# First gather of an expert stage: index from three groups, rows scaled by GpSimd and stored in halves, one score matrix from rounded products

## The reference

```
h = layernorm(x) * (1 + ca) + sa
x = x + ga * attention(h)      # softmax inside segments of 128 rows, plus a global part over segment heads
h = layernorm(x) * (1 + cb) + sb
score = softmax(h @ Wg + bg); expert = argmax; gate = max      # 16 experts, 512 slots each
y = relu(h[slot] @ W1[e] + b1[e]) @ W2[e] + b2[e]
x = x + gb * where(kept, y * gate, 0)      # a token past its expert's 512 slots gives 0
```

## Time and profile before

| what | value |
|---|---|
| three runs | 1816.24 us median, 1816.03 to 1816.32 |
| profiled execution, on the device | 1814.79 us |
| its span, first to last instruction | 1813.2 us |
| mean granted clock of PE | 0.995 of full |
| PE busy | 1779.8 us (98%) |
| PE weight loads busy | 1489.6 us (82%) |
| DVE busy | 1112.3 us (61%) |
| ACT busy | 893.4 us (49%) |
| POOL busy | 610.1 us (34%) |

### The profile page before, as it was taken

How to read it: one execution, slowest core, us unless ns; L and a number is a source line. 1 busy time by engine, 2 the same in 40 slices (tenths; PEclk the granted TensorE clock), 3 DMA queues, 4 the chain that set the end, 5 groups by cost and what they waited for, 6 DMA issues and landing times.

```text
span 1813.2 us, 27903 instructions
## 1 busy us (share of the span) xinstructions
PE 1779.8 (98%) x9135; PEld 1489.6 (82%) x9136; DVE 1112.3 (61%) x1964; ACT 893.4 (49%) x1317; POOL 610.1 (34%) x565
## 2 busy tenths in 40 slices
PE   9999999999999799999999999998998999999998
PEld 5788888888888488898888888888888888888886
DVE  6577887887887644445445444457558675444753
ACT  4446546546546344354444444347467664434741
POOL 1145555555554511123030303043225431304303
PEclk9999999999999899999999999999999999999999
DMA  7586767777777454344453524265446553426522
GB/s 278 183 228 186 197 157 204 180 173 200 188 193 221 95 174 160 112 168 167 144 169 107 174 98 162 98 207 197 158 141 225 197 212 129 155 98 211 201 80 79
DMA packets 148429, 304.09 MB, mean 168 GB/s; under 512 B 18097, under 2 KB 18493, under 8 KB 146326
## 3 DMA queue, kind: packets, MB, share of 16 engines
q1 hardware_dynamic: 115098, 221.01, 35.0%
q0 software_dynamic: 33280, 82.42, 18.8%
HBM read 254.29 MB, written 67.43 MB: 177 GB/s over the span
## 4 chain that ended last, share of the span: by engine, by line
PE 89%; DVE 1%; ACT 1%; issue 1%; DMA 1%; POOL 0%; POOLq 0%; ACTq 0%; DVEq 0%
PE bank L344 27%; PE bank L346 27%; PE bank L345 27%; PE bank L778 3%; PE bank L962 1%; PE bank L875 1%; PE bank L649 1%; PE bank L770 1%; DMA h_rows<-xr 1%; ACT h_f L1304 0%; PE bank L753 0%; ACT h_hi L1303 0%; PE bank L748 0%; DVE w_lo L1746 0%; PE bank L785 0%
## 5 line engine op out<-in xcount | busy, mean ns | idle before, releaser
L1303 ACT ACTIVATE h_hi<-bank,b_col 128x512 fp32r<-128x512 f32 x256 | 176.8, 691 | 526.1 <-PE bank L346 474.9
L1773 DVE TENSOR_TENSOR h_lo<-h_f,h_hi 128x512 fp32r<-128x512 f32 x256 | 174.0, 691 | 349.9 <-ACT h_f L1304 270.7
L344 PE MATMUL bank<-bt_hi,w_hi 128*128 128x512 f32 (+4 forms) x1024 | 359.1, 351 | 3.9 <-DVE w_lo L1746 3.5
L345 PE MATMUL bank<-bt_lo,w_hi 128*128 128x512 f32 (+4 forms) x1024 | 358.0, 350 | 0.0
L346 PE MATMUL bank<-bt_hi,w_lo 128*128 128x512 f32 (+4 forms) x1024 | 358.0, 350 | 0.0
L344 PE MATMUL bank<-w_hi,h_hi 128*128 128x512 f32 x832 | 325.8, 392 | 1.0 <-issue 1.0
L345 PE MATMUL bank<-w_lo,h_hi 128*128 128x512 f32 x832 | 324.2, 390 | 0.0
L346 PE MATMUL bank<-w_hi,h_lo 128*128 128x512 f32 x832 | 323.9, 389 | 0.0
L2069 POOL DMA_INDIRECT out_dram<-yo,tok_x x64 | 75.4, 1178 | 671.7 <-DVE yo L1808 636.4
L344 PEld LDWEIGHTS bank<-bt_hi,w_hi 128*128 128x128 f32 x1024 | 193.2, 189 | 28.8 <-issue 5.6
L345 PEld LDWEIGHTS bank<-bt_lo,w_hi 128*128 128x128 f32 x1024 | 193.3, 189 | 21.2 <-issue 0.2
(11 more groups left out here) (312 smaller groups left out, 2938.0 us busy)
## 6 DMA issues: line engine op xcount, KB each, us to landing
raw<-in_L_ffn_W_dram SPq DMA_DIRECT2D x128, 1024.0 KB
xa<-in_L_attn_x_dram SPq DMA_DIRECT2D x16, 1024.0 KB, 8.5
xr<-in_L_attn_x_dram SPq DMA_DIRECT2D x16, 1024.0 KB, 6.8
xr<-global_rows POOLq DMA_DIRECT2D x16, 1024.0 KB, 8.6
h_rows<-sb_tab SPq DMA_DIRECT2D x16, 1024.0 KB
out_dram<-xr SPq DMA_DIRECT2D x16, 1024.0 KB, 10.7
h_rows<-h POOLq DMA_DIRECT2D x15, 1024.0 KB
b_bc<-in_L_ffn_b_dram SPq DMA_DIRECT2D x16, 256.0 KB, 6.3
```

The lines of the kernel that those rows point to most:

```text
L344: pe.matmul(o, a_hi, b_hi, start=start, stop=False)
L345: pe.matmul(o, a_hi, b_lo, start=False, stop=False)
L1303: act.activation(h1_hi[b % 2][:, j, :], h_bank[j][:, :], ACT.Relu, bias=bias)
L1773: dve.tensor_tensor(h1_lo[b % 2][:, j, :], h1_f[:, j, :], h1_hi[b % 2][:, j, :].bitcast(F32), ALU.subtract) \
```

## The change

Four parts. The score matrix is made from rounded products: ACT rounds each slice of Wk and Wq as it lands, DVE subtracts, PE makes 48 rounded matmuls instead of 16 plain ones, with eight warm-up matmuls instead of six; DVE's splits of M wait for all four copies, since M's parts lie where the rounded Wq lay. The lookup on chip covers Z2, Z1 and Z, so the table's part for expert 0 is loaded before Z2 is scattered, and ahead of SP's last output store; empty entries hold T (8192), and the constants are chosen so that the index is one addition. POOL scales the last group's rows and stores them in two halves, and all scatters of Z2, Z1 and Z follow the first gather. PE makes the ranks of Z1 between two pairs of router quarters.

```diff
     KEY_STEP = 1 << 14
-    FIRST_TAB = 11
-    SPLIT_WV, SPLIT_M, SPLIT_WO, SPLIT_V = 0, KC, 2 * KC, 3 * KC
+    FIRST_TAB = 16
+    NO_TOKEN = T
+    SPLIT_WV, SPLIT_M, SPLIT_WO, SPLIT_V = 2 * KC, 3 * KC, 4 * KC, 5 * KC
...
         load_w2((0, 1), 1)
-        iteration(Group(NG // 2, 0), False, True, False)
-        for par in range(2):
-            sp.wait_ge(scattered[par], 16 * GS * (NG // 2 - 1))
+        sp.wait_ge(scattered[Z3.par], 16 * GS * (Z3.half + 1))
+        sp.wait_ge(scattered[Z2.par], 16 * GS * Z2.half)
...
         sp.dma_start(first_tab[:], slots[:, 0, :, :]).then_inc(first_in, 16)
+        iteration(Group(NG // 2, 0), False, True, False)
...
         pe.wait_ge(ident_made, 2)
-        for _ in range(6):
+        for _ in range(8):
...
         for k in range(KC):
-            pe.wait_ge(wqk_in[k], 32)
+            pe.wait_ge(pro_hi_done, 2 * k + 2)
             for c in range(KC):
-                last = pe.matmul(pro_bank(MCH + c)[:, :], wq_s[:, k, chunk(c)], wk_s[:, k, :],
-                                 start=(k == 0), stop=(k == KC - 1))
+                pe.matmul(pro_bank(MCH + c)[:, :], wq_hi[:, k, chunk(c)], wk_hi[:, k, :], start=(k == 0), stop=False)
+            pe.wait_ge(split_made, 2 * k + 2)
+            for c in range(KC):
+                pe.matmul(pro_bank(MCH + c)[:, :], wq_hi[:, k, chunk(c)], wk_lo[:, k, :], start=False, stop=False)
+                last = pe.matmul(pro_bank(MCH + c)[:, :], wq_lo[:, k, chunk(c)], wk_hi[:, k, :], start=False,
+                                 stop=(k == KC - 1))
...
                 pe.matmul(bank[:, :], ident[:], ga_tab[:, 0, :], start=True, stop=True)
-        def quarters(g):
+        def quarters(g, between=lambda: None):
             for k in range(KC):
+                if k == KC // 2:
+                    between()
...
                 for s in range(GS):
-                    last = pe.matmul(t1_last[:, 0:2 * GS], first_sel[:, which, s, :],
-                                     first_pick[:, which, s, :, :].rearrange("p a j -> p (a j)"), start=(which == 0 and s == 0),
-                                     stop=(which == 1 and s == GS - 1))
-                if which == 1:
+                    for part in range(2):
+                        last = pe.matmul(t1_last[:, 0:GS], first_sel[:, which, s, :], first_pick[:, which, s, part, :],
+                                         start=(which == 0 and s == 0 and part == 0),
+                                         stop=(which == 2 and s == GS - 1 and part == 1))
+                if which == 2:
...
                         last.then_inc(h2t_full, 1)
-            ranks(Z1)
-            quarters(Z)
+            quarters(Z, lambda: ranks(Z1))
...
             first_slots(0)
+            first_slots(1)
             ranks(Z)
-            first_slots(1)
+            first_slots(2)
...
             act.activation(dst, src, ACT.Copy, scale=scale).then_inc(pro_evac, 1)
+        for k in range(KC):
+            act.wait_ge(wqk_in[k], 32)
+            act.activation(wk_hi[:, k, :], wk_s[:, k, :], ACT.Copy).then_inc(pro_hi_done, 1)
+            act.activation(wq_hi[:, k, :], wq_s[:, k, :], ACT.Copy).then_inc(pro_hi_done, 1)
...
         for k in range(KC):
-            act.activation(wv_hi[:, k, :], wv_s[:, k, :], ACT.Copy).then_inc(wv_hi_done, 1)
+            act.activation(wv_hi[:, k, :], wv_s[:, k, :], ACT.Copy).then_inc(pro_hi_done, 1)
...
             dve.memset(quad_sum[k * QUAD:k * QUAD + 1, :], 1.0).then_inc(init_made, 1)
+        for k in range(KC):
+            dve.wait_ge(pro_hi_done, 2 * k + 1)
+            dve.tensor_tensor(wk_lo[:, k, :], wk_s[:, k, :], wk_hi[:, k, :].bitcast(F32), ALU.subtract) \
+                .then_inc(split_made, 1)
+            dve.wait_ge(pro_hi_done, 2 * k + 2)
+            dve.tensor_tensor(wq_lo[:, k, :], wq_s[:, k, :], wq_hi[:, k, :].bitcast(F32), ALU.subtract) \
+                .then_inc(split_made, 1)
...
         for k in range(KC):
-            dve.wait_ge(wv_hi_done, k + 1)
+            dve.wait_ge(pro_hi_done, 2 * KC + k + 1)
...
                 .then_inc(split_made, 1)
+        dve.wait_ge(pro_evac, MCH + KC)
...
             dve.wait_ge(first_step, f + 2)
-            dve.tensor_scalar(first_pick[:, which, :, 0, :], first_tile[:], place[:, 2 * GS:2 * GS + 1], None, ALU.mult) \
+            dve.tensor_scalar(first_pick[:, which, :, 0, :], first_tile[:], place[:, 3 * GS:3 * GS + 1], None, ALU.mult) \
...
         def first_index():
-            dve.wait_ge(first_in, 16)
-            dve.tensor_copy(first_f[:, 0, :], first_tab[:, :, 0]).then_inc(first_step, 1)
-            row, segment = t1_last[:, 0:GS], t1_last[:, GS:2 * GS]
-            shift, whole, total = first_f[:, 1, :], first_f[:, 2, :], first_f[:, 3, :]
             dve.wait_ge(first_full, 1)
-            dve.tensor_scalar(shift, row, 0.0, float(Z1.n * ROWS - 1 - NO_TOKEN), ALU.is_gt, ALU.mult) \
-                .then_inc(first_step, 1)
             dve.wait_ge(first_step, FIRST_TAB)
-            dve.scalar_tensor_tensor(out=whole, in0=segment, scalar=float(P), in1=first_f[:, 0, :], op0=ALU.mult,
-                                     op1=ALU.add).then_inc(first_step, 1)
-            dve.wait_ge(first_step, FIRST_TAB + 2)
-            dve.tensor_tensor(total, row, whole, ALU.add).then_inc(first_step, 1)
-            dve.wait_ge(first_step, FIRST_TAB + 3)
-            dve.tensor_tensor(tok_h[:], shift, total, ALU.add).then_inc(tok_h_ready, 1)
+            dve.tensor_tensor(tok_h[:], t1_last[:, 0:GS], first_f[:, 0, :], ALU.add).then_inc(tok_h_ready, 1)
...
                 first_rows(g, which)
+            if which == 2:
+                dve.wait_ge(first_in, 16)
+                dve.tensor_copy(first_f[:, 0, :], first_tab[:, :, 0]).then_inc(first_step, 1)
...
                 .then_inc(route, 1)
+            if which == 2:
+                first_index()
...
             dve.tensor_tensor(count[:], count[:], osum[:], ALU.add).then_inc(route, 1)
-            if which == 1:
-                first_index()
...
             dve.tensor_tensor(xr[Z.par][:, s, :], xr[Z.par][:, s, :], big[s][:, :], ALU.add).then_inc(x2_ready, 1)
-        def scale_rows(s):
-            dve.wait_ge(xn2_done, 4 * Z.n + s + 1)
-            dve.tensor_tensor(xr[Z1.par][:, s, :], h2[Z.par][:, s, :], cb_tab[:, batch_of(Z), :], ALU.mult) \
-                .then_inc(h2_ready, 1)
...
             half_stats(Z, 2)
-            route_slots(Z2)
-            dve.wait_ge(x2_stored[Z1.par], 16 * (Z1.half + 1))
+            route_slots(Z2, 0)
             route_logits(Z1)
-            for s in range(GS):
-                scale_rows(s)
-            route_slots(Z1, 0)
+            route_slots(Z1, 1)
             route_logits(Z)
-            route_slots(Z, 1)
+            route_slots(Z, 2)
...
             gather(xh, h2_dram, tok_h, xh_in)
-        def store_h2(g, rows=None):
+        def store_h2(g):
...
             stand_alone(pool, pool_passed)
-            rows = h2[g.par] if rows is None else rows
-            pool.dma_start(group_rows(h2_dram, g), rows[:], accum_op=ALU.add).then_inc(h2_stored[g.par], 16)
+            pool.dma_start(group_rows(h2_dram, g), h2[g.par][:], accum_op=ALU.add).then_inc(h2_stored[g.par], 16)
...
                       allow_small_or_imprecise_dtypes=True).then_inc(made, 1)
-            pool.iota(place[:, 0:2 * GS], pattern=[[1, 2 * GS]], base=0, channel_multiplier=0,
+            pool.iota(place[:, 0:3 * GS], pattern=[[P, 3 * GS]], base=Z2.n * ROWS - NO_TOKEN, channel_multiplier=0,
                       allow_small_or_imprecise_dtypes=True).then_inc(made, 1)
-            pool.iota(place[:, 2 * GS:2 * GS + 1], pattern=[[0, 1]], base=1, channel_multiplier=1,
+            pool.iota(place[:, 3 * GS:3 * GS + 1], pattern=[[0, 1]], base=0, channel_multiplier=1,
...
                 pool.tensor_tensor(NR2[:, both], MN2[:, both], RS2[:, both], ALU.mult).then_inc(ln2_rstd, 1)
-            scatter(Z2)
-            store_h2(Z, xr[Z1.par])
-            for par in range(2):
-                pool.wait_ge(h2_stored[par], 16 * (NG // 2))
+            scaled = xr[Z1.par]
+            pool.wait_ge(x2_stored[Z1.par], 16 * (Z1.half + 1))
+            pool.wait_ge(shift_stored[Z.par], 16 * (Z.half + 1))
+            for lo in (0, 2):
+                for s in (lo, lo + 1):
+                    pool.wait_ge(xn2_done, 4 * Z.n + s + 1)
+                    pool.tensor_tensor(scaled[:, s, :], h2[Z.par][:, s, :], cb_tab[:, batch_of(Z), :], ALU.mult) \
+                        .then_inc(h2_ready, 1)
+                pool.wait_ge(h2_ready, 4 * Z.n + lo + 2)
+                pool.dma_start(group_rows(h2_dram, Z)[:, lo:lo + 2, :], scaled[:, lo:lo + 2, :], accum_op=ALU.add) \
+                    .then_inc(h2_stored[Z.par], 16)
+            pool.wait_ge(h2_stored[Z1.par], 16 * (Z1.half + 1))
+            pool.wait_ge(h2_stored[Z.par], 16 * (Z.half + 2))
...
             gather_h(0)
+            pool.wait_ge(first_in, 16)
+            scatter(Z2)
```

14 lines of the change are left out of this document (8 added, 6 removed).

## The result

The changed kernel takes 1833.14 us (median of 5 runs, 1832.17 to 1833.77) against 1816.32 (5 runs, 1816.03 to 1817.07): a ratio of 1.0092, 95% interval 1.0078 to 1.0106. The prediction was 1814.8, with a range up to 1817.2, and gave 5% to "slower". The profiled execution has a span of 1831.6 us and a device time of 1833.14, with PE's mean granted clock at 0.989 of full (0.995 before). The profiled execution of before took 1814.79 us, less than any of its timed runs (1816.03 to 1817.07).

What follows compares the result with a forecast made beforehand. TensorE, busy for 98% of the span, was taken as the bound. Prologue 0 plus tail 1.4 us took the span from 1813.2 to 1811.8 and the median from 1816.24 to 1814.8 us, range 1812.3 to 1817.2.

Steps and rivals of the forecast that it cites:

- Prologue, 0: Rounded score matrix: PE done 2.4 us earlier, all lost waiting for the second modulation matrix; gain 0.
- (b): Prologue rival: the second modulation matrix lands with PE, or earliness pays otherwise; 2.4 + 1.4 us, 1812.4; 6%.
- (d): Prologue loses: DVE late costs up to 1 us, or clock drop costs 2 to 3.4; 1815.3 to 1818.2; 9%.
- What PE gets of it: Before expert 0's transposes: keep-busy starts at 612.6, not 613.31, gather hidden; gain 1.4 us, bounds 0.67 and 2.1.
- Tail, on DVE, and store and gather: Tail: 2.49 us of scaling leaves DVE for POOL, index ready at 611.2, gather at 612.1 instead of 615.65.
- The stores: Tail: second half store issued at 603.1, against 604.69 for the whole, landed at 609, upper end 613.2.
- Keep-busy: Ahead of the first transposes: its six records still take 4.97 us, ending at 617.6.
- What is queued behind: Twelve scatters after the gather end at 637.9, next weight block issued at 641.6; slack 3.8 us, costs nothing.
- Rival (e): Table and weight block come late behind twelve scatters; 1830.8 if each scatter is as long as the slowest; 3%.
- (a): Tail rival: PE's full clock returns earlier, during keep-busy; gain 2.8 us, 1813.4; 10%.

Runs made afterwards that it cites:

- e4: The kernel before with the rounded score matrix alone: 1817.01 us, ratio 1.0005.
- e2: As e1, with the last group's scaling back on DVE: 1818.76 us, ratio 1.0017.
- e3: The changed kernel with Z2 scattered ahead of POOL's multiplications and stores, as in the kernel before: 1823.01 us, ratio 1.0039.
- e10: As e7, with the lookup in one multiplication of eight columns, as before the change, and two additions for the index: 1815.50 us, ratio 0.9994.
- e1: The changed kernel with slot and payload buffers of its own for Z, without the wait on Z2's scatters: 1822.66 us, ratio 1.0044.
- e8: As e1, with POOL's four operations reading one input (times 1.0), the batch-row scale left out: 1819.07 us, ratio 1.0016.
- e12: As e11, with one store of the last rows instead of two halves: 1817.71 us, ratio 1.0007.
- e7: As e2, with two keep-busy multiplications instead of three: 1820.82 us, ratio 1.0027.
- e9: As e7, with the score matrix as before the change: 1816.19 us, ratio 1.0003.
- e11: As e9, with e10's lookup in one multiplication of eight columns: 1815.48 us, ratio 0.9996.
- e5: The kernel before with 99 more PE instructions, waits long met, in three idle stretches: 1822.98 us, ratio 1.0040.
- e6: As e2, with 156 more PE instructions, waits long met, in three idle stretches: 1824.12 us, ratio 1.0047.

## Why the prediction was wrong, point by point

- **Prologue, 0.** Right in the mean. PE was done at 17.5 and waited for the second modulation matrix, as the forecast had it, but for 1.35 us (to 21.32) and not 2.3; the next matrix started at 24.86 instead of 25.32 because the load landed that much sooner. e4 measured 1.0005 for the part alone. Behind the mean stand both rivals, each in the profiles of some kernels, since the load does not land at one time. In e4's profile it was there by 20.34, and the next matrix started at 23.89, 1.4 us sooner than before: half of (b). In those of e2, e3 and e10 PE waited 2.12, 2.02 and 3.02 us, the clock fell right behind, and the next matrix started at 26.44, 26.43 and 27.79, 1.1 to 2.5 us later than before: that is (d). e10's timeline and windows of PE:

```profile
22.54 0.59 PE L607 MATMUL bank<-wk_s,bias_col 128*1 128x512 f32 x1 [3.02 <-DMA wm_b<-in_L_wmod_dram]
```

```profile
24.00:27.00 3.00, 3.00 (x20) 0.71 (x16) 2.90 (x7) 0.00 (x0) 0.00 (x0) 0.50 0.51 95
```

- **What PE gets of it.** This is the step that failed. It said of DVE's last routing step, for which the count and the keep-busy matmuls wait, that it "moves by 0.4" (and 0.3 by the shorter index), to the better. I had listed the waits that the diff adds, and what queues behind the scatters on POOL and SP, but not who else waits for a scatter: the wait on `scattered[g.par]` stands in `route_slots` unchanged, and the change moves what meets it from ahead of the gather to behind it. The 13.96 us on PE are worth 10.5 us of the time (e1). It could have been seen ahead: the forecast had the gather at 612.1 and gave each gather instruction 1.3 us and each scatter 1.72 in working out when the scatters end, so by its own terms Z2's four were done near 624, some 12 us behind the step that waits for them.
- **Tail, on DVE, and store and gather.** This is the second term that was mis-sized. The sum took 2.49 us off DVE and gave POOL its 5 us at no price to DVE. The price is some 5.4 us on DVE, and 3.6 to 3.9 us of the time (e8, e2 against e1). I had cited the rule that the two engines share interfaces only for POOL's side. Another page of the Trainium skill (SBUF — State Buffer, SBUF: two separate sides) states it for both: the pair goes to one of them for the whole of an instruction, when VectorE is in one of its two-port modes, or reads two SBUF inputs while GpSimd reads SBUF. By that rule, the trace agrees with the lengths (1.27 and 1.21 us beside multiplications of 1.26), with the instructions that read PSUM, but not with the third, 3.46 us, which began ahead of POOL's operation and was held over two of them, and not with e8, where GpSimd's operations of 1.5 us, which also read SBUF, cost DVE's instructions 0.4 us. The trace of before already had both cases. Its DVE timeline beside POOL's multiplications of 555.77 (1.29 us) and 582.73, where the short one is held to the end of the multiplication and the two with an input in PSUM take their 0.69 each:

```profile
556.25 0.83 DVE L1624 SCALAR_TENSOR_TENSOR per_tok<-per_tok 128x4 f32<-128x4 f32 x1
...
582.78 1.29 DVE L1658 TENSOR_TENSOR bank<-bank,ga_tab 128x512 f32<-128x512 f32 x2
```

- **The stores.** The half stores went as said: issued at 599.25 and 603.30, and in time; e12 shows that they matter once the scatters are behind the gather.
- **Keep-busy.** Its 4.97 us were 4.77; right. With the tail mended it is what the transposes wait for: two instead of three let them start at 617.17 (e7) instead of 619.38 (e2), of which 0.8 us is an earlier start of keep-busy.
- **What is queued behind.** Right in kind: the table was issued at 640.28, and nothing of the experts waited for it. Rival (e) did not come: the twelve scatters took 1.43 us each (621.96 to 639.09), less than the 1.72 forecast, and one alone was long (2.90 us, beside a subtraction of DVE's). As for (a), the clock did not come back sooner.
- **Not in any step:** the change lengthens PE's program by 72 instructions. That costs the gap of 2.58 us and the low clock behind it, 4.2 us in the profile; e10, which takes it away together with the third keep-busy multiplication, is 3.3 us under e2, and 5.3 under e7, which has that multiplication out and the gap in.

10.5, 3.9 and 3.3 us, from the changed kernel by e1 and e2 to e10, are the 17.6 us from 1833.14 to 1815.50; by the intervals of the runs each step is uncertain by some 2 to 4 us. The intervals of e9 to e12 against before all hold 1: no version here was shown to be faster than the kernel before.

Open: why e11 has a gap at 667 with four instructions more than before, and why a head start of 2 to 3 us at the transposes (e9, e11) is gone by the end of the span. Part of it is the gaps at code transfers near 667 and 714 (in e9 1.04 and 1.30 us, where before has none and 0.99), in e11 part is low clock in the experts' loop; no run separates them. Single profiles also differ there by the clock: eleven of the fourteen have a stretch of 3.4 us at the lower level that begins between 1247 and 1262, and before, e9 and e11 have none; theirs are the three shortest spans (1813.2, 1813.2 and 1813.5). No edit sorts them, since e11 and e12 differ in the store alone, so 1 to 2 us between the spans of two profiles say little.

## What to carry to other kernels

When work is moved in a queue, look up every wait on what it signals in the whole kernel, not only the waits in the diff: a buffer shared by parity ties the group that moves to one two groups on. Ask what an operation moved to GpSimd does to VectorE's short instructions while it runs, before counting what it frees there. And a gap at a jump that nothing released may be a matter of where the code lies, as here; it can be tested by instructions that do nothing (count them from the records, since one product of the source can be two of them), and it can hide what an edit is worth.

## What the runs showed of the hardware

- GpSimd's two-input multiplications of 1.26 to 1.5 us held off VectorE's instructions of 0.14 to 0.23 us to their end, over two multiplications in three cases (3.46 us in the changed kernel, 3.10 and 3.52 in e3), a copy with one SBUF input among them (3.52). With one input on GpSimd the same instructions took 0.23 to 0.62 us (e8).
- PE stood for 2.3 to 3.3 us at a jump in its program in seven kernels, with the DMA share at 0.44 (e5) as at 1.00 (the changed kernel), and did not stand at 1.06 (e10). Behind it the granted clock was 0.50 to 0.55 of full for some 3 us in the changed kernel, e2 and e5 and for twice that in e7, and stayed at 1.00 in e1, e3 and e8.
- A wait long met costs PE time: 99 instructions made of them, 33 in each of three stretches that were idle for 0.6 to 2.9 us before, put keep-busy off by 3.7 us (e5). The stretches with 33, 36 and 60 of them lasted 3.40, 3.66 and 6.22 us (e5, e6), so some 0.10 us for one with two waits.
- The 1 MB load `wm_b` took 12.2 us from issue to landing in e4, 13.9 in before and 14.3 in e10, with the same loads ahead of it. Behind PE's waits for it of 2.02 to 3.02 us in e2, e3 and e10 the clock fell to the lower level for 3.4 us; behind 2.47 and 2.53 us in e7 and e1 it did not.
